# Attention over 1,601 keys on one core: score, maxima and small products in strips of 32 rows in three of four head groups, key packs loaded by head

## The reference, cut to what matters

```
q = (norm(x) @ Wq).reshape(256, 16, 8)
k = (ctx @ Wk).reshape(keys, 16, 8);  v likewise       # keys = 1601 (cross) or 256 (self)
s = einsum('qhd,khd->hqk', q, k) / sqrt(8)
o = einsum('hqk,khd->qhd', softmax(s), v)
x = x + o @ Wp
```

## Time and profile before

| | us |
|---|---|
| median of 3 runs | 6480.61 (6472.38 to 6483.08) |
| the profiled execution | 6475.3 |
| its span in the trace | 6473.5 |
| mean granted TensorE clock | 0.98 |

### The profile page before, as it was taken

How to read it: one execution, slowest core, us unless ns; L and a number is a source line. 1 busy time by engine, 2 the same in 40 slices (tenths; PEclk the granted TensorE clock), 3 DMA queues, 4 the chain that set the end, 5 groups by cost and what they waited for, 6 DMA issues and landing times.

```text
span 6473.5 us, 147216 instructions
## 1 busy us (share of the span) xinstructions
PE 5939.3 (92%) x49714; PEld 3112.4 (48%) x49714; DVE 4119.5 (64%) x6523; ACT 4237.2 (65%) x8158; POOL 981.5 (15%) x1660
## 2 busy tenths in 40 slices
PE   6999999999877899999999977789999999999998
PEld 3444444444444444544454444444444444445665
DVE  5767677677555667766776445467777777754443
ACT  3777777777666577777777556557777777773333
POOL 3121121121111111111111011212212212200000
PEclk9999999999999899999999989899999999999999
DMA  2322322222111322232232011122232232220110
GB/s 88 78 65 56 79 59 63 75 56 69 42 57 61 82 68 65 69 79 69 57 76 75 1 57 57 55 77 68 57 77 68 57 77 68 57 65 21 54 53 29
DMA packets 180915, 402.05 MB, mean 62 GB/s; under 512 B 16992, under 2 KB 124560, under 8 KB 166416
## 3 DMA queue, kind: packets, MB, share of 16 engines
q1 hardware_dynamic: 180752, 400.01, 22.9%
HBM read 316.81 MB, written 83.14 MB: 62 GB/s over the span
## 4 chain that ended last, share of the span: by engine, by line
PE 73%; issue 8%; ACT 8%; DVE 7%; DMA 2%; SPq 1%; POOL 1%; ACTq 0%; DVEq 0%; POOLq 0%
PE bank L1140 19%; PE bank L1186 18%; PE pair L1156 14%; DVE MX L1480 3%; PE bank L1112 2%; ACT P L1316 2%; PE bank L1107 2%; DMA QP<-scr_q 2%; PE pair L1173 2%; PE pair L1162 1%; PE bank L699 1%; PE bank L690 1%; ACT QP L1327 1%; PE pair L626 1%; DVE ST L1437 1%
## 5 line engine op out<-in xcount | busy, mean ns | idle before, releaser
L1316 ACT ACTIVATE P<-bank 128x512 f32<-128x512 f32 (+1 forms) x5504 | 3102.2, 597 | 1350.6 <-PE bank L1140 1306.9
L1480 DVE TENSOR_REDUCE MX<-pair 128x2 f32<-128x802 f32 x3072 | 2923.9, 988 | 1296.3 <-PE pair L1156 1288.0
L1140 PE MATMUL bank<-QP,KP 128*128 128x256 bf16 (+1 forms) x11008 | 2091.3, 277 | 141.7 <-ACT P L1316 90.0
L1186 PE MATMUL bank<-P,VA 128*25 128x256 f32 (+1 forms) x22016 | 1756.0, 391 | 5.8 <-issue 0.5
L1156 PE MATMUL pair<-KP,QP 96*128 96x401 bf16 x6144 | 1576.0, 338 | 60.9 <-DMA QP<-scr_q 42.3
L1140 PEld LDWEIGHTS bank<-QP,KP 128*128 128x128 bf16 (+1 forms) x11008 | 858.0, 100 | 1577.3 <-ACT P L1316 912.9
L1186 PEld LDWEIGHTS bank<-P,VA 128*25 128x25 f32 (+1 forms) x22016 | 401.7, 102 | 711.0 <-issue 456.7
L1156 PEld LDWEIGHTS pair<-KP,QP 96*128 96x128 bf16 x6144 | 593.5, 98 | 181.7 <-DVE MX L1480 64.0
L1605 POOL COPY VA<-VN 128x416 f32<-128x416 f32 (+1 forms) x320 | 138.6, 434 | 2520.6 <-PE bank L1186 2439.1
L1484 DVE TENSOR_REDUCE MX<-pair 128x4 f32<-128x1024 f32 x256 | 311.3, 1223 | 326.8 <-PE pair L1162 326.2
L1327 ACT CAST QP<-pair 2x512 bf16<-2x512 f32 x640 | 338.9, 575 | 130.1 <-PE pair L1173 124.7
(11 more groups left out here) (246 smaller groups left out, 4497.5 us busy)
## 6 DMA issues: line engine op xcount, KB each, us to landing
KP<-scr_k SPq DMA_DIRECT2D x192, 900.6 KB
QP<-scr_q SPq DMA_DIRECT2D x960, 48.0 KB
CN<-ctx_n SPq DMA_DIRECT2D x40, 768.0 KB
scr_k<-KSF SPq DMA_DIRECT2D x48, 600.8 KB, 3.3
scr_k<-KSF SPq DMA_DIRECT2D x48, 600.0 KB, 3.3
CT<-ctx_t SPq DMA_DIRECT2D x24, 800.5 KB, 4.4
KP<-scr_ks SPq DMA_DIRECT2D x128, 144.0 KB
scr_q<-QS SPq DMA_DIRECT2D x80, 192.0 KB, 2.1
```

What stands on the lines that cost most here:

```text
L1140: last = nc.tensor.matmul(SC[half][0:kt, k * N:(k + 1) * N], KP[g][:, c0:c0 + kt], QP[g][:, h * N:(h + 1) * N], start=True, stop=True)
L1186: last = nc.tensor.matmul(OB[32 * h:32 * h + STEP + HD + 1, 0:N], VA[g % 2][0:kt, t, h, :], P[(g * ph.nt + t) % 2][0:kt, h * N:(h + 1) * N ...
L1316: nc.scalar.activation(P[v % 2][0:kt, half * 2 * N:(half + 1) * 2 * N], SC[half][0:kt, :], ACT.Exp, scale=SCALE).then_inc(sem("probs_full" ...
L1480: nc.vector.tensor_reduce(MX[:, r, c:c + 2], MP[j % 2][:, :].rearrange("p (t k) -> p t k", t=2)[:, :, 0:SPANS[0][1]], AX.X, ALU.max).then_ ...
```

## The change

The products of `scores`, `maximum` and the pieces (other than the transposes and "mean") go through a helper that cuts the output rows into strips of `cols`; with 128 it issues the one product as before. `cols` is 32 in groups two to four of a cross element, and 128 in group one and in self elements. The value products and the shift rows are untouched. In every attention phase the key pack is loaded by four transfers, one for each head, and the wait counts seven loads (112).

```diff
-            **{"packed_loaded%d" % g: 64 for g in range(NG)}), B)
+            **{"packed_loaded%d" % g: 112 for g in range(NG)}), B)
...
-                    sp.dma_start(KP[g][0:R9, 0:G * ph.nk],
-                                 kscr[:, G * g:G * g + G, :].rearrange("r h k -> r (h k)").unsqueeze(1).to_broadcast(
-                                     [3 * HD, 3, G * ph.nk])).then_inc(sem("packed_loaded%d" % g), 16)
+                    for h in range(G):
+                        sp.dma_start(KP[g][0:R9, h * ph.nk:(h + 1) * ph.nk],
+                                     kscr[:, G * g + h, :].unsqueeze(1).to_broadcast([3 * HD, 3, ph.nk])).then_inc(
+                            sem("packed_loaded%d" % g), 16)
...
+            def strips_of(cols, out, lhsT, rhs, start=True, stop=True):
+                n = lhsT.shape[1]
+                for c in range(0, n, cols):
+                    m = min(cols, n - c)
+                    last = nc.tensor.matmul(out[c:c + m, :], lhsT[:, c:c + m], rhs, start=start, stop=stop)
+                return last
...
-                    last = nc.tensor.matmul(SC[half][0:kt, k * N:(k + 1) * N], KP[g][:, c0:c0 + kt],
-                                            QP[g][:, h * N:(h + 1) * N], start=True, stop=True)
+                    last = strips_of(cols, SC[half][0:kt, k * N:(k + 1) * N], KP[g][:, c0:c0 + kt],
+                                     QP[g][:, h * N:(h + 1) * N])
...
-                    pe.wait_ge(sem("packed_loaded%d" % g), at("packed_loaded%d" % g, b, 64))
+                    pe.wait_ge(sem("packed_loaded%d" % g), at("packed_loaded%d" % g, b, 112))
...
-                        last = nc.tensor.matmul(MP[j % 2][:, k * 512:k * 512 + n],
-                                                QP[g][0:MR, h * N + qt * 128:h * N + qt * 128 + 128],
-                                                KP[g][0:MR, h * ph.nk + c0:h * ph.nk + c0 + n], start=True, stop=True)
+                        last = strips_of(cols, MP[j % 2][:, k * 512:k * 512 + n],
+                                         QP[g][0:MR, h * N + qt * 128:h * N + qt * 128 + 128],
+                                         KP[g][0:MR, h * ph.nk + c0:h * ph.nk + c0 + n])
...
-                        scores(ph, b, g, t, 0)
+                        cols = 32 if ph.cross and g > 0 else 128
+                        scores(ph, b, g, t, 0, cols)
```

More of the change, by code:

```diff
@@ L1076, in _, with piece @@
             pe.wait_ge(sem("cleared"), 1)
-            def piece(el, role, name):
+            def strips_of(cols, out, lhsT, rhs, start=True, stop=True):
[4 more added lines that the diff above has]
+                return last
+            def piece(el, role, name, cols=128):
                 if name in NO_BANK:
@@ L1090, in piece @@
                     pe.wait_ge(sem("squared"), at("squared", b, 1))
-                    last = nc.tensor.matmul(MISC[:, 0:N], w("mean"), SQ[:, 0:N], start=True, stop=True)
+                    last = strips_of(cols, MISC[:, 0:N], w("mean"), SQ[:, 0:N])
                 elif name == "q":
@@ L1094, in piece @@
                     pe.wait_ge(sem(done), at(done, b, 1))
-                    last = nc.tensor.matmul(MISC[:, 0:N], w(ph.name + "wq"), XM[:, 0:N], start=True, stop=True)
+                    last = strips_of(cols, MISC[:, 0:N], w(ph.name + "wq"), XM[:, 0:N])
                     if not ph.cross:
-                        last = nc.tensor.matmul(MISC[:, N:2 * N], w(ph.name + "wk"), XM[:, 0:N], start=True, stop=True)
+                        last = strips_of(cols, MISC[:, N:2 * N], w(ph.name + "wk"), XM[:, 0:N])
                 elif name[0] == "t":
@@ L1106, in piece @@
                         pe.wait_ge(sem("ctx_loaded"), at("ctx_loaded", b, 16))
-                    last = nc.tensor.matmul(MISC[:, 0:n], w(ph.name + "wk"), CT[:, c0:c0 + n], start=True, stop=True)
+                    last = strips_of(cols, MISC[:, 0:n], w(ph.name + "wk"), CT[:, c0:c0 + n])
                 elif name[0] == "v":
@@ L1111, in piece @@
                         kt = ph.tiles[t]
-                        last = nc.tensor.matmul(MISC[0:kt, k * D:(k + 1) * D], src[:, t * 128:t * 128 + kt],
-                                                w(ph.name + "wv"), start=True, stop=True)
+                        last = strips_of(cols, MISC[0:kt, k * D:(k + 1) * D], src[:, t * 128:t * 128 + kt], w(ph.name + "wv"))
                 elif name == "d":
@@ L1116, in piece @@
                     for c in range(2 * NPAIR):
-                        last = nc.tensor.matmul(MISC[:, c * 2 * G:(c + 1) * 2 * G], RS[:, c * 128:(c + 1) * 128], w("pick"),
-                                                start=True, stop=True)
+                        last = strips_of(cols, MISC[:, c * 2 * G:(c + 1) * 2 * G], RS[:, c * 128:(c + 1) * 128], w("pick"))
                 elif name == "e":
@@ L1121, in piece, with scores @@
                     for c in range(2 * NPAIR):
-                        last = nc.tensor.matmul(MISC[:, c * 128:(c + 1) * 128],
-                                                RDX[:, c * 128:(c + 1) * 128], w("ident"), start=True, stop=True)
+                        last = strips_of(cols, MISC[:, c * 128:(c + 1) * 128], RDX[:, c * 128:(c + 1) * 128], w("ident"))
                 elif name == "y":
                     for p in range(NPAIR):
-                        last = nc.tensor.matmul(MISC[:, 0:N], w(ph.name + "wp", p * D, D), ON[:, p * N:(p + 1) * N],
-                                                start=(p == 0), stop=(p == NPAIR - 1))
+                        last = strips_of(cols, MISC[:, 0:N], w(ph.name + "wp", p * D, D), ON[:, p * N:(p + 1) * N],
+                                         start=(p == 0), stop=(p == NPAIR - 1))
                 last.then_inc(sem("misc_full"), 1)
-            def scores(ph, b, g, t, half):
+            def scores(ph, b, g, t, half, cols):
                 at, kt = ph.c.at, ph.tiles[t]
@@ L1139, in scores, with maximum @@
                     c0 = h * ph.nk + t * 128
[L1140 to L1141 removed]
+                    last = strips_of(cols, SC[half][0:kt, k * N:(k + 1) * N], KP[g][:, c0:c0 + kt],
+                                     QP[g][:, h * N:(h + 1) * N])
                 last.then_inc(sem("scores_full"), 1)
[L1144 removed]
+            def maximum(ph, b, g, j, cols=128):
                 at = ph.c.at
                 if j == 0:
[L1148 removed]
+                    pe.wait_ge(sem("packed_loaded%d" % g), at("packed_loaded%d" % g, b, 112))
                 elif j == 1:
@@ L1161, in maximum @@
                         for qt in range(2):
-                            last = nc.tensor.matmul(MP[j % 2][:, (2 * k + qt) * N:(2 * k + qt + 1) * N],
-                                                    QP[g][0:MR, h * N + qt * 128:h * N + qt * 128 + 128],
-                                                    KP[g][0:MR, h * ph.nk:(h + 1) * ph.nk], start=True, stop=True)
+                            last = strips_of(cols, MP[j % 2][:, (2 * k + qt) * N:(2 * k + qt + 1) * N],
+                                             QP[g][0:MR, h * N + qt * 128:h * N + qt * 128 + 128],
+                                             KP[g][0:MR, h * ph.nk:(h + 1) * ph.nk])
                 last.then_inc(sem("max_full"), 1)
@@ L1199, in element @@
                         among, behind = el.here(g * ph.nt + t)
-                        scores(ph, b, g, t, 0)
+                        cols = 32 if ph.cross and g > 0 else 128
+                        scores(ph, b, g, t, 0, cols)
                         for j in js[:third]:
-                            maximum(*ahead, j)
+                            maximum(*ahead, j, cols)
                         for piece_ in among:
-                            piece(el, *piece_)
-                        scores(ph, b, g, t, 1)
+                            piece(el, *piece_, cols)
+                        scores(ph, b, g, t, 1, cols)
                         for j in js[third:2 * third]:
-                            maximum(*ahead, j)
+                            maximum(*ahead, j, cols)
                         if last_tile:
```

## The result

The change takes 6683.6 us (median of 4 runs, 6661 to 6699) where the kernel before takes 6481.8 beside it: a ratio of 1.031, interval 1.0283 to 1.0337. It is 3.1% slower; forecast was 2.3% faster, and the range ended at 6,460. The profiled execution took 6661.4.

The account below looks back on a forecast made before the run. TensorE was taken as the bound, busy 92% of the span, with dead time at switches to and from strips. From 6475.3: -244 + 13 + 75 + 8 = -148, 6327, as a median 6332 us; range 6,245 to 6,460.

Parts of the forecast that it names:

- -223: Cross phases and phase starts: 244 us gained by strips, less 13 for late packs and 8 for starts of phases.
- Strips side by side, issue cheap: TensorE's strip slots in cross phases: four strips stream together, extra starts cost nothing, 0.22 us saved a slot.
- rivals 1 and 2: Strip slots: bf16 strips don't run side by side, 7,650 us, 9%; instruction issue is the bound, 7,200 us, 6%.
- The gain of 244 us in the cross phases: Strip groups two to four: 308 us saved, less 38 for ScalarE behind key pieces and 26 for context transposes.
- 8 by starts of phases: Extra pack-load issues at five phase starts, 1.6 us each: 8 us lost.
- My friction: VectorE's maxima in strip groups, 94% taken but not the bound: 0.15 us allowed a group.
- So starts are cheap and I price them at nothing: Cross batches: about 858 extra instruction pairs each on TensorE, priced at zero, covered by 0.107 us of streaming.
- rival 3: TensorE's loop turns: doubled body no longer stays in instruction memory, 1.8 to 3.6 us a turn, 110 taken, 6440; 12%.
- Packs by head, cross phases: 13 us lost: Four pack loads ahead of query loads in cross phases should just fit; 0.3 us in each of 45 batches.
- Packs by head, self phases: 75 us: Three more issues ahead of the awaited query load: 2.5 us longer in each of 30 self batches, 75 us lost.
- Rivals 4 and 5: Packs late in cross phases, 2 us in 45 batches, 6,420, 10%; extra issues free in self batches, 6,255, 6%.

Follow-up runs that it names:

- the written-out version: Strips in groups two to four, packs by head in cross phases only, TensorE's cross loops written out without branch back, against the kernel before: 6294.3 us, 0.9724.
- The experiment with few bytes: Strips with cross loops written out and packs by head there, loads within a cross phase bringing 64 keys of each head instead of 1,601: 6260.4 us, 0.9666.

## Why the prediction was wrong

By the experiments the loss is made up so: strips, by head in the cross phases, no loop -182 us; the loop +289; by head in the self phases +100; together +207, and 6683.6 - 6476.4 is 207 (6476.4 is the kernel before beside these runs). The forecast had -223, nothing, and +75.

*Strips side by side, issue cheap:* right, the slot rows above (a slot with two maxima 1.56, forecast 1.58); rivals 1 and 2 are out.

*The gain of 244 us in the cross phases, 13 of it given back by the packs, and 8 by starts of phases:* mis-sized a little, 196 of 223. A c1 batch written out went from 93.8 to 89.3 on average (88.4 to 92.0). What went beyond my allowances is ScalarE: over the middle of c1 in the written-out version, TensorE waited for probabilities 53.9 us in 94 places, where it had been 25.1 in 43. My friction was laid on VectorE, which held.

*"So starts are cheap and I price them at nothing":* this is the step that failed. The start of an instruction is cheap, but it has to be there. I counted 858 additional pairs a batch and asked only what TensorE needs to start them, not what it takes to bring them in. As rival 3 the matter had 12% and a price of 76 to 151 us for 42 turns (39 of them have a branch back). It was 289 for the loop alone, for two reasons. A turn took 2.9 to 5.2 us of branch instead of 1.8 to 3.6, and TensorE went to the lower clock behind it: in c1 a batch of the loop had 9.6 us idle and 88.4 busy, written out 5.2 and 84.3, so half of the 8.5 us is clock. And the waits inside the body were not among my steps at all: a block of 256 instructions lasted some 13 us of work before and lasts some 5 in strips, and the next read isn't always there by then. A wait ends 2.3 to 3.0 us after the start of its read, and what is late is that start. At best it came 0.7 us after a branch's end; after waits in the body it came up to 4 us later in the changed kernel, and up to 8 us later with pack loads of one piece.

*Packs by head, cross phases: 13 us lost* by waits for late loads. The sign was wrong. Those waits are 2.6 us inside all three cross phases of the changed kernel; written out they are 13 us, but 31 with one load. With loads by head the reads came sooner, worth 217 us in the loop, 209 written out. What it is in a row's size that frees them (the time a packet holds its engine, 862 or 173 ns, is the candidate) was not isolated from the number and the times of the loads. The experiment with few bytes only says that in short rows the bytes are a small part, 34 us.

*Packs by head, self phases: 75 us:* right in kind, 100 measured. The wait grew by 2.4 us, as reckoned (2.5); but a batch grew by 3.3, and the rest is the 6 us at clock 0.57 behind the longer wait. I had priced the wait and not what comes behind it. This too is read from windows, not isolated by a run.

*Rivals 4 and 5:* the packs were not late in the cross phases (2.6 us), and the extra issues were not free, by the run with loads by head only.

## What to carry to other kernels

Before cutting instructions into more and smaller ones, look how many a loop's body holds and what the instruction queue moves: if it moves nearly nothing, the bodies stay loaded, and that is worth more than it seems; doubled, this one lost 4.5% to being a loop, while the same strips written out won 2.8%. A wait "for issue" in the middle of equal products is a late instruction; look then for what else the DMA engines carry, and in what row size. And a stall on TensorE costs itself and the slow clock after it, here another 0.4 of it (2.4 us of wait in a self batch made it 3.3 us longer) to as much again (the loop's batch above); where an edit makes an idle stretch longer, price both.

## What the runs showed that I had not expected

- A loop's branch depends on where it falls in a block of 256 instructions: 0.35 to 5.2 us for bodies that are read again at each turn, and moving the head alone, with the same code, took 173 us off (6583.3 to 6409.9).
- TensorE's waits for instructions can be seen in the trace, though no semaphore marks them: nearly all end 2.2 to 3.2 us after the start of a 16-KB packet on the instruction queue, and with little else on the DMA engines the next packet starts 0.7 us after the branch. By the sum, an estimate, a read takes 3 to 4 us from entering the block before. That they are read just one block ahead fits all this, but wasn't tested.
- Cutting a load in four by head, which cuts its rows from 12.8 to 3.2 KB with the same bytes, made this kernel 209 to 217 us faster, though hardly anything waited for the load itself, and though it needs 48,000 more packets.
- Eight strips (two products in four) last as long as the two whole products, 0.39 and 0.38 us, but the change to and from them costs 0.1 us each way; 39 slots with 0.22 each are all that strips can win here.
